# First layer's attention: split keys and values kept in DRAM, split score and value products, token-major dense product

## The reference, cut to what matters

```python
# 2 batches of 1024 tokens, 256 features; 16 heads in 4 groups, 128 features a head
q = einsum('bsh,he->bse', x, w_q).reshape(b, sq, GROUPS, HPG, KVC)
k, v = split(einsum('bsh,he->bse', x, w_kv), 2)            # 4 groups of 128 each
scores = einsum('bqgpd,bkgd->bgqpk', q, k) * KVC ** -0.5
scores = where(causal, scores, -inf)
probs = softmax(scores, axis=-1)
ctx = einsum('bgqpk,bkgd->bqgpd', probs, v).reshape(b, sq, HEADS * KVC)
out = einsum('bse,eh->bsh', ctx, w_dense)                  # added to x
```

## Time and profile before

| | us |
|---|---|
| median of 3 runs (lowest to highest) | 3837.56 (3833.1 to 3840.24) |
| profiled execution | 3841.85 |
| span of its trace | 3840.0 |
| PE, DVE, ACT, POOL busy in the span | 3466.9, 2420.7, 1537.1, 1403.2 |
| keys and values (`l0_kv`) | 43.70 to 99.30 |
| the 16 heads (`l0_heads`), 58.02 a head | about 102.8 to 1043.0 |

### The profile page before, as it was taken

How to read it: one execution, slowest core, us unless ns; L and a number is a source line. 1 busy time by engine, 2 the same in 40 slices (tenths; PEclk the granted TensorE clock), 3 DMA queues, 4 the chain that set the end, 5 groups by cost and what they waited for, 6 DMA issues and landing times. The chain is left out here.

```text
span 3840.0 us, 66211 instructions
## 1 busy us (share of the span) xinstructions
PE 3466.9 (90%) x21608; PEld 2618.4 (68%) x21608; DVE 2420.7 (63%) x4872; ACT 1537.1 (40%) x2827; POOL 1403.2 (37%) x1083
## 2 busy tenths in 40 slices
PE   6899999999889799999997759999859999699997
PEld 4677777777666688888884335555438888388883
DVE  3556556555433566566665668989468888488883
ACT  2444444444332444444443215666333333233332
POOL 1323333333222566666663320000013444544444
PEclk8999999999999899999998888999979999899998
DMA  0000000000100100000000222222034443144431
GB/s 34 8 4 4 5 3 5 5 3 5 36 0 0 54 18 14 18 18 18 17 16 3 96 110 78 83 82 80 25 115 107 115 115 97 36 107 115 114 97 48
DMA packets 120727, 183.19 MB, mean 48 GB/s; under 512 B 22545, under 2 KB 69777, under 8 KB 120337
## 3 DMA queue, kind: packets, MB, share of 16 engines
q1 hardware_dynamic: 114512, 173.90, 15.0%
q0 software_dynamic: 6144, 8.39, 1.3%
HBM read 153.80 MB, written 28.18 MB: 47 GB/s over the span
## 5 line engine op out<-in xcount | busy, mean ns | idle before, releaser
L447 POOL TENSOR_TENSOR l0h_probs<-l0h_probs,l0h_inv 128x128 f32<-128x128 f32 (+7 forms) x256 | 292.7, 1146 | 586.1 <-DVE l0h_inv L482 586.1
L1798 DVE TENSOR_REDUCE l2h_half<-l2h_s 128x1 f32<-128x512 f32 x512 | 337.5, 686 | 47.5 <-PE l2h_s L1700 46.7
L378 PE MATMUL l0h_sc<-l0a_KT,l0h_QT 128*128 x768 | 298.2, 501 | 29.2 <-ACT l0h_probs L551 27.5
L1785 ACT ACTIVATE l2h_PT<-l2h_s 128x1024 f32<-128x1024 f32 x256 | 248.3, 1022 | 162.4 <-PE l2h_s L1710 162.3
L405 PE MATMUL l0h_cx<-l0h_PT,l0h_VG 128*128 128x128 f32 x2304 | 300.7, 276 | 0.0
L551 ACT ACTIVATE l0h_probs<-l0h_sc,l0h_negtop 128x128 f32<-128x128 f32 (+7 forms) x256 | 189.6, 741 | 245.3 <-DVE l0h_negtop L477 244.8
L405 PEld LDWEIGHTS l0h_cx<-l0h_PT,l0h_VG 128*128 128x128 f32 x2304 | 278.1, 192 | 1.0
L159 POOL TENSOR_TENSOR XN<-XN,n_rstd 128x512 f32<-128x512 f32 x32 | 39.8, 1266 | 595.1 <-DVE n_rstd L140 595.1
L1700 PE MATMUL l2h_s<-l2h_K,l2h_Q 128*128 128x512 f32 x512 | 218.8, 466 | 22.6 <-DMA l2h_K<-l_split 20.3
L475 DVE TENSOR_REDUCE l0h_top<-l0h_sc 128x1 f32<-128x128 f32 (+7 forms) x256 | 194.1, 758 | 8.8
L378 PEld LDWEIGHTS l0h_sc<-l0a_KT,l0h_QT 128*128 128x128 f32 x768 | 126.0, 192 | 106.0 <-issue 63.5
(11 more groups left out here) (407 smaller groups left out, 9017.2 us busy)
## 6 DMA issues: line engine op xcount, KB each, us to landing
l3p_decb<-l_decays SPq DMA_DIRECT2D x128, 256.0 KB, 4.5
l3p_w<-L_w SPq DMA_DIRECT2D x34, 512.0 KB, 3.7
l2h_Q<-l_split SPq DMA_DIRECT2D x64, 256.0 KB
l2h_K<-l_split SPq DMA_DIRECT2D x64, 256.0 KB
l3p_prow<-l_decays SPq DMA_DIRECT2D x128, 128.0 KB, 3.2
l_split<-l2q_hi SPq DMA_DIRECT2D x16, 512.0 KB, 4.0
l_split<-l2q_lo SPq DMA_DIRECT2D x16, 512.0 KB, 3.8
l3p_wgu<-L_ffn_w_gate_up SPq DMA_DIRECT2D x32, 256.0 KB, 4.8
```

The lines of the kernel that those rows point to most:

```text
L378: mm = pe.matmul(sc[u % 2][:, lo:lo + n], QT[:, u * P:(u + 1) * P], KT[:, ds(g, 1), b * S + lo:b * S + lo + n], start=True, stop=True)
L447: pool.tensor_tensor(p, p, inv[:, u % 4:u % 4 + 1].to_broadcast([P, keys(u)]), ALU.mult).then_inc(probs_scaled, 1)
L1785: act.activation(PT[:, b, kb, :], s2[kb % 2][:, :], ACT.Exp, scale=L2_SCALE).then_inc(exped, 1)
L1798: dve.reduce_max(half[:, b, t, z:z + 1], bank(slot_of(i))[:, :], AX_X).then_inc(s1_read, 1)
```

## The change

Keys and values are split into fp32r high and low parts as they are made (ACT copies the high part, DVE subtracts it), staged in four buffers and stored by SP in two DRAM tensors. V jobs now come first. After job 20 the first group is read back to `KH`, `KL`, `VH`, `VL`, the other groups at the group borders. Scores and value products become three fp32r products each, the latter for two units at once (256 columns wide, their last block 128). Every turned tile is taken by two engines: ACT copies the high part to `PTH`, DVE subtracts to `PTL`. So are the queries, 1024 wide (`QH` by ACT, `QL` by DVE).

The slots run on across heads without a drain: 18 a head, 16 for the units in the order t = 0, 1, 6, 7, 2, 3, 4, 5 of each batch, and slots 4 and 13, in which PE makes the queries of a batch that is next needed. POOL no longer divides; the dense product, now token-major (context turned as weights, all of `w_dense` in SBUF), is multiplied by the inverse sum on DVE and added to `acc`, 128 tokens by 256 features for each of 16 blocks. After the last head 32 transposes bring `acc` back to features by tokens, and eight DVE additions put it into `XT`. The maximum is negated in the reduction. Outside `l0_attn` and its parts nothing changes.

```diff
-        jobs = [("k", g, j) for g in range(L0_GROUPS) for j in range(NJ)] + [("v", t, 0) for t in range(TT)]
+        jobs = [("v", t, 0) for t in range(TT)] + [("k", g, j) for g in range(L0_GROUPS) for j in range(NJ)]
+        FIRST = TT + NJ
...
+                for n in range(len(jobs)):
+                    if n == FIRST:
+                        for i in range(NB):
+                            sp.wait_ge(stored[i], 32 * (FIRST // NB))
+                        for b in range(B):
+                            load_keys(sp, kd, kv, 0, b)
+                            load_values(sp, vd, kv, 0, b)
+                    sp.wait_ge(hi_ready, n + 1)
+                    sp.dma_start(target(n, 0), staged(hi, n)).then_inc(stored[n % NB], 16)
+                    sp.wait_ge(lo_ready, n + 1)
+                    sp.dma_start(target(n, 1), staged(lo, n)).then_inc(stored[n % NB], 16)
...
+    UNITS = [(b, t) for b in range(B) for m in (0, 3, 1, 2) for t in (2 * m, 2 * m + 1)]
+    SLOTS = [("unit", i) for i in range(4)] + [("query", 1)] + [("unit", i) for i in range(4, 12)] + [("query", 0)] + [("unit", i) for i in range(12, 16)]
...
+                        end = L0_HPG * g + L0_HPG - 1
+                        sp.wait_ge(scores_ready, NU * end + NQ)
+                        load_keys(sp, kd, kv, g + 1, 0)
+                        sp.wait_ge(pv_done, NPAIR * end + NPAIR // B)
+                        load_values(sp, vd, kv, g + 1, 0)
+                        sp.wait_ge(scores_ready, NU * end + NU)
+                        load_keys(sp, kd, kv, g + 1, 1)
+                        keys_arrived(g + 1, 0)
...
-                                mm = pe.matmul(sc[u % 2][:, lo:lo + n], QT[:, u * P:(u + 1) * P],
-                                               KT[:, ds(g, 1), b * S + lo:b * S + lo + n], start=True, stop=True)
+                        pe.matmul(sc[s % 2][:, lo:lo + n], QH[:, q], kv.KH[:, key], start=True, stop=False)
+                        pe.matmul(sc[s % 2][:, lo:lo + n], QH[:, q], kv.KL[:, key], start=False, stop=False)
+                        mm = pe.matmul(sc[s % 2][:, lo:lo + n], QL[:, q], kv.KH[:, key], start=False, stop=True)
...
-                                mm = pe.matmul(cx[:, 0:P], VG[:, b * NQ + kb, :], PT[:, u % 2, kb, :], start=(kb == 0), stop=(kb == t))
+                        pe.matmul(cx[:, col], kv.VH[:, V, :], PTH[:, pair % 2, kb, col], start=(kb == 0), stop=False)
+                        pe.matmul(cx[:, col], kv.VH[:, V, :], PTL[:, pair % 2, kb, col], start=False, stop=False)
+                        mm = pe.matmul(cx[:, col], kv.VL[:, V, :], PTH[:, pair % 2, kb, col], start=False, stop=(kb == t))
...
+                            pe.wait_ge(pt_lo, NT * h + n - 1)
...
+                    if i or not isinstance(h, int) or h > 0:
+                        pe.wait_ge(added, NU * h + i)
+                    pe.matmul(outp[:, 0:D], ctxT[:, i // 2 % 2, i % 2 * P:(i % 2 + 1) * P], wd[:, ds(h, 1), :].rearrange("p a n -> p (a n)"),
+                              start=True, stop=True).then_inc(dense_done, 1)
...
+                        kind, i = SLOTS[s]
+                        if kind == "unit":
+                            bank_free(h, s)
+                            scores(h, s, i)
+                        elif exists(h + 1 - i):
+                            bank_free(h, s)
+                            project(h + 1 - i, i, sc[s % 2])
+                    if u := unit_at(h, s, 2):
+                        turn_probs(*u)
+                    if u := unit_at(h, s, 5):
+                        dense(*u)
+                    if (u := unit_at(h, s, 3)) and u[1] % 2:
+                        weigh_values(*u)
...
+                    dve.scalar_tensor_tensor(out=QL[:, q], in0=bank[:, :], scalar=L0_SCALE, in1=QH[:, q].bitcast(F32),
+                                             op0=ALU.mult, op1=ALU.subtract).then_inc(ql_ready, 1)
...
+                        dve.tensor_tensor(PTL[part], tp[n % 2][:, 0:m * P].rearrange("p (m n) -> p m n", m=m), PTH[part].bitcast(F32),
+                                          ALU.subtract).then_inc(pt_lo, 1)
...
+                    dve.scalar_tensor_tensor(out=x, in0=outp[:, 0:D], scalar=inv[:, i % 8:i % 8 + 1], in1=x, op0=ALU.mult, op1=ALU.add).then_inc(added, 1)
...
+                            row_max(h, s, i)
+                        elif exists(h + 1 - i):
+                            low_queries(2 * h + (3 if i == 0 else 2), i, sc[s % 2])
+                    if u := unit_at(h, s, 2):
+                        invert(*u)
+                        low_probs(*u)
+                    if u := unit_at(h, s, 5):
+                        add_dense(*u)
```

More of the change, by code:

```diff
@@ L321, in l0_heads @@
         tp = [st.ps(f"tp{i}") for i in range(2)]
[L322 to L335, removed]
+        cx, outp = st.ps("cx"), st.ps("outp")
+        wq_loaded, wd_loaded, whi_ready, wlo_ready = st.sem("wq_loaded"), st.sem("wd_loaded"), st.sem("whi_ready"), st.sem("wlo_ready")
+        keys_here, values_here = [st.sem(f"keys_here{b}") for b in range(B)], [st.sem(f"values_here{b}") for b in range(B)]
@@ new lines, in back, with exists, unit_at, steps @@
+        def back(h, s, n):
+            return (h, s - n) if s >= n else (h - 1, s - n + NS)
+        def exists(h):
+            return not isinstance(h, int) or 0 <= h <= LAST
+        def unit_at(h, s, n):
+            hh, ss = back(h, s, n)
+            kind, i = SLOTS[ss]
+            return (hh, i) if kind == "unit" and exists(hh) else None
+        def steps(engine, step):
+            for s in range(NS):
+                step(0, s)
+            with engine.Fori(1, LAST) as h:
+                for s in range(NS):
+                    step(h, s)
+            for s in range(NS):
+                step(LAST, s)
+            for s in range(5):
+                step(LAST + 1, s)
@@ new lines, in group @@
+                def group(g, last):
+                    for i in range(L0_HPG):
+                        h = L0_HPG * g + i
+                        if not last or i < L0_HPG - 1:
+                            sp.wait_ge(wlo_ready, h + 1)
+                            query_weights(h + 1)
+                    if not last:
+                        end = L0_HPG * g + L0_HPG - 1
[6 more added lines that the diff above has]
+                        keys_arrived(g + 1, 0)
+                        values_arrived(g + 1, 0)
+                        sp.wait_ge(pv_done, NPAIR * end + NPAIR)
+                        load_values(sp, vd, kv, g + 1, 1)
+                        keys_arrived(g + 1, 1)
+                        values_arrived(g + 1, 1)
@@ L352, in _, with project @@
+                for b in range(B):
+                    keys_arrived(0, b)
+                    values_arrived(0, b)
+                with sp.Fori(0, L0_GROUPS - 1) as g:
+                    group(g, False)
+                group(L0_GROUPS - 1, True)
             @block.tensor
             def _(pe):
-                def project(h, pieces):
+                def project(h, b, bank):
                     pe.wait_ge(wlo_ready, h + 1)
[L357 to L360, removed]
@@ new lines, in _ @@
+                project(0, 0, sc[1])
+                steps(pe, step)
+                for n in range(NJ * DC):
+                    j, c = divmod(n, DC)
+                    pe.wait_ge(added, NU * L0_HEADS)
+                    wait(pe, x_added, n - 3)
+                    bank = sc[n // 2 % 2][:, n % 2 * BANK:(n % 2 + 1) * BANK]
+                    for i in range(4):
+                        mm = pe.transpose(bank[:, i * P:(i + 1) * P], acc[:, 4 * j + i, c * P:(c + 1) * P], k.ident[:, :])
+                    mm.then_inc(turned_back, 1)
```

400 lines of the change are left out of this document (200 added, 200 removed).

## The result

The change makes the kernel slower by 1.1%: 3877.65 us against 3835.94 for the kernel before (medians of 4 runs each; ratio 1.0108, 95% interval 1.009 to 1.0125). The forecast was 3954. The sign and the places of the longest waits came out as foretold, the size did not: +42 us where +116 was forecast.

The account below looks back on a forecast made before the run. PE was taken to bound the heads, with short waits. Heads +83, keys and values +21, start and drain +3, additions back +6.5, borders +2 make 116 on 3841.85; less 4.3 for the median, 3954, range 3925 to 3985.

Parts of the forecast that it names:

- The price of narrow products: PE's 128-wide fp32r products in the heads: 0.222 us each, 0.11 as the other end; PE's work 52.3 a head.
- the forecast's own first rival: Heads: 128-wide fp32r products at 0.11, the load's pace; work 48.3, waits up to 12.2, period 60.5, total 3910; chance 0.27.
- The waits: PE waiting in the heads for DVE's low parts and additions: 4.05 a projection, 2.8 in other slots, 10.9 a head.
- of the 6.0 before none stays: Heads: the 6.0 us a head beyond PE's priced work in the kernel before was all waits, and would go.
- Keys and values: Stage of keys and values: DMA's bytes take 61.7 us plus some 3 for landings, ending at 120.3 against 99.0, +21.
- The ends: Before and after the heads: start and last drain +3 together, eight additions into `XT` +6.5.
- Start, drain and borders: Start and last drain of the heads +3 together, key and value loads at three group borders +2.
- The chain that PE hides: Rival, heads: the chain behind each projection is covered, PE's 52.3 a head alone bounds; 3778, deciding below 56.0; chance 0.17.
- Products 256 wide at the f32 rate: Rival, value products and scores: 256-wide fp32r products take 0.444 each, 550 more, about 4500; chance 0.04.
- V stores at half rate: Rival, stage of keys and values: V stores go at half rate, +28 more, 3982; chance 0.05.

Follow-up runs that it names:

- e10: e4's kernel with the three 128-wide fp32r value products of each pair issued twice; 3790.15 us, ratio 0.9878 to the kernel before.
- e4: Changed kernel without DVE's subtraction for the probabilities' low part; PE multiplies the high part twice; 3765.54 us, ratio 0.9802 to the kernel before.
- e2: Changed kernel with the first group's keys and values written straight into their tiles, not stored or read back; 3862.5 us, ratio 1.006 to the kernel before.
- e5: Changed kernel with eight staging buffers for the stores in place of four; 3876.08 us, ratio 1.0109 to the kernel before.
- e11: e2's kernel with the low parts of keys and values neither stored nor read back; 3856.86 us, ratio 1.0053 to the kernel before.
- e7: Changed kernel with DVE's order in each slot made addition, tiles' low parts, then queries' low part; 3819.04 us, ratio 0.9958 to the kernel before.

## Why the prediction was wrong in size

- **The price of narrow products** was the first step that failed: "I take 0.222 and keep 0.11 as the other end". It took the f32 product of that width as the row to go by; e10 measures 0.106, and the trace has 0.29 for three. With 36 such products a head that is 36 × 0.11 = 4.0 of PE's work, 64 us over 16 heads; by the forecast's own first rival, 60.5 for 63.2, the waits would have taken 1.3 of each 4.0 back. The row of the transposes had the price: a transpose leaves one record, as an fp32r product does, and an f32 product two. By the Trainium skill ("TensorE: Matmul & The Clock Gate", section "LDWEIGHTS (loading the stationary operand)") a weight load takes its columns over 1.2, in ns; for 128 columns I estimate 107 from it, and e10's 0.106 us agrees.
- **The waits** stand where the prediction put them, behind each projection, for `PTL` and then for the addition, but PE loses less to them: 1.92 + 0.48 and 1.94 + 0.95 for twice 4.05, and 5.9 a head in all for 10.9 (12.2 in the rival with narrow products at the load's pace). The step that failed added up DVE's durations: counted from the projection's start, the forecast has `QL` begin at 5.57 and the addition end at 11.6; the trace has 5.50 and 10.7. DVE's timeline in the change:

```profile
356.71 1.23 DVE L573 SCALAR_TENSOR_TENSOR l0h_QL<-l0h_sc,l0h_QH 128x1024 fp32r<-128x1024 f32 x1 [3.42 <-ACT l0h_QH L628]
357.85 0.15 DVE L578 RECIPROCAL l0h_inv<-l0h_total 128x1 f32<-128x1 f32 x1
357.92 1.14 DVE L587 TENSOR_TENSOR l0h_PTL<-l0h_tp,l0h_PTH 128x512 fp32r<-128x512 f32 x2
358.98 0.48 DVE L595 SCALAR_TENSOR_TENSOR l0h_acc<-l0h_outp,l0h_inv,l0h_acc 128x256 f32<-128x256 f32 x1
359.37 0.29 DVE L566 TENSOR_TENSOR l0h_sc<-l0h_sc,causal 128x128 f32<-128x128 f32 x1
...
360.24 1.27 DVE L587 TENSOR_TENSOR l0h_PTL<-l0h_tp,l0h_PTH 128x512 fp32r<-128x512 f32 x2
361.42 0.47 DVE L595 SCALAR_TENSOR_TENSOR l0h_acc<-l0h_outp,l0h_inv,l0h_acc 128x256 f32<-128x256 f32 x1
```

Most rows end after the next has begun: the addition at 358.98 is listed with 0.48, and the mask starts 0.39 later; the reciprocal at 357.85 has 0.15, and the tiles start 0.07 later. From the queries' start to the end of the last addition the trace has 361.89 − 356.71 = 5.2, the sum 6.0. The Trainium skill ("VectorE: DVE Perf Modes", section "Two Vector instructions with no wait between them") says that a held instruction starts only when every earlier one has finished; by it these instructions, which start 0.08 or 0.09 before the listed end of the one ahead, are not held, and no row here shows one that is. What counts in this queue is the distance of the starts. The small waits at other slots come to 0.6 a head for 2.8; what made them smaller was not followed.
- **Time that is neither a product's price nor a listed wait** was put at nothing by "of the 6.0 before none stays". Already in the kernel before only 58.02 − 54.62 = 3.4 of the 6.0 is idle time; the other 2.6 is busy time beyond the prices. In the change 57.98 − 5.9 = 52.1 stands beside the listed waits, and the work priced with 0.11 is 48.3: 3.8 a head are of this kind. So the 5.2 between forecast and trace, 63.2 − 57.98, are 4.0 for narrow products and 5.0 for waits, less these 3.8. That the head's own 52.3 looks right beside the 52.1 is luck: two errors cancel in it. What the 3.8 are is shown in part only. The clock, 1.00 before and 0.97 here, is 0.3 to 0.7 of them: it fell behind 15 of 31 projections, in the head shown for 3 to 4 us, and half a head with a fall is 28.9 to 29.4 long, without one 28.6 to 28.7. The rest of what a fall costs is hidden under the second wait, which is 0 to 0.5 behind a fall and 0.9 to 1.1 otherwise. The remaining 3 or so are nearly gone in e4 (48.6), so they hang on DVE's subtraction; waits too short for the list would do that, but this was not shown.
- **Keys and values** were forecast at +21 and came to +30.6. The mechanism, bytes over DMA's pace, held (e2, e5, e11). The sum had 61.7 + 3, the trace 71.4 (20.97 MB at 294 GB/s). It had V at 300 GB/s, where windows of the trace 2 us long have 287 or so. It left out that SP, before it reads the first group back, waits for all stores to land; DMA's share falls to 0.16 meanwhile. Windows in the V stores, at that wait and in the last K stores, and SP's issues:

```profile
61.60:63.60 2.00, 2.00 (x10) 1.67 (x9) 1.20 (x2) 0.69 (x2) 0.00 (x0) 1.00 1.03 287
...
95.60:97.60 2.00, 2.00 (x10) 1.67 (x9) 1.27 (x2) 0.70 (x2) 0.00 (x0) 1.00 0.16 30
...
123.60:125.60 2.00, 0.00 (x0) 0.00 (x0) 0.69 (x1) 0.60 (x1) 0.00 (x0) 0.50 1.04 397
```

```profile
91.61 0.65 SPq L302 DMA_DIRECT2D l_k<-l0kv_lo  x1
96.39 0.34 SPq L251 DMA_DIRECT2D l0a_KH<-l_k  x1
```

Between the store at 91.61 and the load at 96.39 SP issues nothing. PE's first job also comes 2.0 later (54.04 for 52.02). The V stores go in pieces of 512 bytes at some 287 GB/s with DMA's share at 1.03, the last K stores in pieces of 2 KB at up to 397. The Trainium skill ("DMA: Bandwidth & Descriptors", section "Specifications") has 512 bytes as the least piece that goes at line rate; the measurement has these stores a quarter below those of 2 KB.
- **The ends**: the additions back took 5.6 (6.5 forecast). Start, drain and borders, +5 forecast, gave 938.1 − 16 × 57.98 = 10.4 where the kernel before has 940.1 − 16 × 58.02 = 11.8, so −1.4.
- **The rivals**: narrow products at the load's pace is what happened, and its 3910 was still 32 too high: its head of 60.5, with waits of 12.2, is 57.98 with 5.9. The chain that PE hides did not occur here. Its threshold, a head of 56.0, is passed in e7 (54.3), which does end below the kernel before, by 0.4%; the rest of its shorter heads is spent on the stage of keys and values. PE's own work, 52.3 in that rival, is 48.6 by e4. Products 256 wide at the f32 rate are ruled out by their 0.12, V stores at half rate by their 287 GB/s.

## What to carry to other kernels

When an operation has no row, look for a row with the same number of records and loads: here it had the price, and the row of the same width and a like name had twice it. Add up a queue by the distances of the starts, not by durations, which made the chain here some 15% too long. Hold the sum of the prices against the busy time as well as against the whole: what is left between them does not vanish with the waits. And when a change lightens the engine that bounds, look at the order on the engine that it then waits for: two steps moved on DVE were worth 58 us here, more than the change had cost.

## What was not expected of the hardware

- One wait of 1.9 us on PE in a busy stretch was followed, within 1.3 us of its end, by the lower clock level, 1.2 GHz (window 359.90 to 362.80 at 0.54). Behind each of the heads' 31 later projections PE waits 1.9 to 2.5 for `PTL`, yet only 15 had a fall: every second one, but for the first two, which both had it, and for those at 380.57 and 409.19, which both had none. What decides it was not tried.
- 128-wide fp32r products come at 0.106, and 256-wide ones at 0.12: halving the width below 256 saves almost nothing.
- The reloads of a group's keys and values at the three borders, 4.2 MB each, cost PE 0.6 us of waits in 15 heads (1.3 in e4 and in e7).
